# A Mamba-style block with a feed-forward on one core: when h, the second statistics, the ReLUs and y's transposes are issued

## The reference, cut to what matters

```python
x: (4, 4096, 512) float32;  D = 512, N = 16 states
mod = (silu(c) @ wmod).reshape(4, 6, 1, 512)      # sa, ca, ga, sb, cb, gb; ga, gb kept away from 0
h   = layernorm(x) * (1 + ca) + sa
x   = x + ga * attn(h)
h   = layernorm(x) * (1 + cb) + sb
x   = x + gb * ffn(h)

def attn(x):
    x_ssm, z = split(x @ w_in.T + b_in)
    z  = silu(z)
    dt = softplus(x_ssm @ w_dt.T + b_dt);  B = x_ssm @ w_B.T + b_B;  C = x_ssm @ w_C.T + b_C
    for every t:  s = exp(A * dt[t]) * s + dt[t] * B[t] * x_ssm[t];  y[t] = sum over N of s * C[t]
    y  = (y + D * x_ssm) * z
    return layernorm(y @ w_out.T + b_out + x) * gamma + beta

def ffn(x):
    s = x @ Win + bin                              # 64 columns
    g = sum over 16 inner units of relu(s * W1 + b1) * W2 + b2
    return g @ Wout + bout
```

## Time and profile before

| | us |
|---|---|
| median of three runs | 5229.29 |
| the profiled execution | 5223.79 |
| its span, first to last instruction | 5222.0 |
| PE busy, share of the span | 4803.0, 92% |
| ACT busy | 3842.9, 74% |
| DVE busy | 3730.8, 71% |
| POOL busy | 3372.6, 65% |
| mean granted TensorE clock | 0.968 |

### The profile page before, as it was taken

One profiled execution on the slowest core, in us unless ns is written; L12 is line 12 of the kernel. 1 busy time (PEld: TensorE's weight loads), 2 busy tenths in 40 slices (PEclk: granted clock), 3 DMA queues, 4 the chain that ended last, 5 costly groups with the idle time before them and its releaser, 6 DMA issues. The chain is left out here.

```text
span 5222.0 us, 76452 instructions
## 1 busy us (share of the span) xinstructions
PE 4803.0 (92%) x25664; PEld 3246.3 (62%) x25664; DVE 3730.8 (71%) x5163; ACT 3842.9 (74%) x6371; POOL 3372.6 (65%) x2699
## 2 busy tenths in 40 slices
PE   5889999999999999999999999999999999999997
PEld 3566666666666666666666666666666666666665
DVE  2577777777777777777777777777777777777775
ACT  0677877777877777877777777778777778777775
POOL 0566666666676666676666666666666666666674
PEclk8999999999999999999999999999999999999999
DMA  3111111111111111111111111111111111111111
GB/s 121 41 45 51 45 45 43 51 50 53 39 54 45 51 52 53 37 51 43 51 51 53 43 49 43 52 51 50 40 44 56 53 51 45 44 43 51 51 45 39
DMA packets 140649, 258.70 MB, mean 50 GB/s; under 512 B 18593, under 2 KB 18593, under 8 KB 140258
## 3 DMA queue, kind: packets, MB, share of 16 engines
q1 hardware_dynamic: 140258, 253.82, 15.4%
HBM read 216.01 MB, written 37.75 MB: 49 GB/s over the span
## 5 line engine op out<-in xcount | busy, mean ns | idle before, releaser
L336 POOL TENSOR_TENSOR work<-work,c_bc 128x512 f32<-128x512 f32 x2048 | 2592.8, 1277 | 1516.7 <-DVE work L1005 1147.5
L1005 DVE TENSOR_TENSOR_SCAN work<-work,state,b_ps 128x512 f32<-128x512 f32 x1792 | 2261.6, 1275 | 648.0 <-PE b_ps L404 605.2
L770 ACT ACTIVATE work<-u_td,b_td 128x512 f32<-128x512 f32 x2048 | 1453.7, 710 | 404.4 <-PE b_ps L404 401.1
L444 PEld LDWEIGHTS y_ps<-ident,work 128*128 128x128 f32 x8192 | 1019.7, 143 | 805.2 <-issue 719.0
L404 PE MATMUL b_ps<-ident,work 128*128 128x128 f32 x8192 | 1276.3, 280 | 250.3 <-DVE work L1005 133.4
L760 ACT ACTIVATE work<-dt_t,neg_a 128x512 f32<-128x512 f32 x2048 | 1451.0, 709 | 45.5 <-DVE work L1005 45.5
L444 PE MATMUL y_ps<-ident,work 128*128 128x128 f32 x8192 | 1234.4, 276 | 0.0
L404 PEld LDWEIGHTS b_ps<-ident,work 128*128 128x128 f32 x8192 | 980.5, 144 | 341.7 <-DVE work L1005 162.8
L596 PE MATMUL dense<-h_t,w_in_t 128*128 128x512 f32 x1024 | 534.3, 614 | 1.1 <-DVE u_td L1086 1.1
L508 PE MATMUL dense<-w_out_t,proj 128*128 128x512 f32 x1024 | 533.1, 614 | 0.0
L535 PE MATMUL dense<-h_t,w_in_t 128*128 128x512 f32 x1024 | 505.6, 597 | 6.6 <-ACT h_t L774 6.1
(11 more groups left out here) (92 smaller groups left out, 4665.6 us busy)
## 6 DMA issues: line engine op xcount, KB each, us to landing
c_bc<-c_d SPq DMA_DIRECT2D x512, 256.0 KB, 3.2
xn<-in_x SPq DMA_DIRECT2D x128, 256.0 KB, 5.0
x<-in_x SPq DMA_DIRECT2D x128, 256.0 KB, 3.7
out_dram<-x SPq DMA_DIRECT2D x128, 256.0 KB, 2.1
work<-in_wmod SPq DMA_DIRECT2D x6, 1024.0 KB, 7.5
par_d<-work SPq DMA_DIRECT2D x4, 768.0 KB, 3.3
w_in_t<-in_w_in_t SPq DMA_DIRECT2D x1, 2048.0 KB, 15.0
gain_shift<-par_d SPq DMA_DIRECT2D x4, 512.0 KB, 4.7
```

Of the source, the lines that this page charges most:

```text
L336: gp.tensor_tensor(pr[:, (s * U + i) % PR_RING, :], hs[:, (s * U + i) % HS_RING, :], c_bc[:, (s * N + n) % C_RING, :], ALU.mult).then_inc( ...
L444: last = mm(y_ps[:, tb, j * P:(j + 1) * P], pr[:, (s * U + i) % PR_RING, tb * P:(tb + 1) * P], ident[:, :], is_transpose=True, start=(i == ...
L770: A(v[:, n % V_RING, tb, :], u_td[:, s % 2, tb, :], ACT.Copy, scale=b_td[:, s % 2, tb, n:n + 1]).then_inc(S["v_done"], 1)
L1005: V.tensor_tensor_scan(hs[:, (s * U + i) % HS_RING, :], decay[:, (s * U + i) % DEC_RING, :], b_ps[:, i % 2, :], state[:, i:i + 1] if s % N ...
```

## The change

Four things move; no instruction that computes is added or removed.

- A semaphore `res_used` is counted up after each `add_residual`. `front`'s h waits for four of these instead of for `pre_ps`.
- `SECOND` becomes units 19, 22, 26, 28.
- `feed_forward` is split: the first two ReLUs of a chunk (`first_relus`) are issued at units 62 and 63 of the step before, the other six at units 0, 0, 1, 2, 2, 3. The last z block's sigmoid moves to units 3, 4, 5, and POOL's `last_gate` to unit 6.
- In `ORDER`, `yz.0` goes ahead of `g.6` and `yz.1` ahead of `g.7`; `dense` follows.

```diff
--- before.py
+++ after.py
@@ -26,7 +26,7 @@
 
 
 
-    ORDER = """g.0 g.1 g.2 g.3 g.4 g.5 g.6 yz.0 g.7 yz.1
+    ORDER = """g.0 g.1 g.2 g.3 g.4 g.5 yz.0 g.6 yz.1 g.7
         res.0 yz.2 pre.0.0 yz.3 pre.0.1 pre.0.2 out.0 pre.0.3
         res.1 pre.1.0 out.1 pre.1.1 pre.1.2 out.2 pre.1.3
         res.2 pre.2.0 out.3 pre.2.1 sk.0 pre.2.2 sk.1 pre.2.3
@@ -63,7 +63,7 @@
         return int(END[".".join(str(n) for n in part)] * U / TOTAL)
 
 
-    SECOND = [made("pre", tb, 3) + 5 for tb in range(TB)]
+    SECOND = [made("pre", tb, 3) + (5 if tb == TB - 1 else 9 - tb) for tb in range(TB)]
 
     ctx = ExitStack()
     with ctx:
@@ -159,7 +159,7 @@
         PER = {
             "SP": dict(stored_0=Q, stored_1=Q, stored_2=Q, stored_3=Q, c_stored=Q),
             "Pool": dict(prod_done=U, xsh_done=TB, x1_done=TB, dt_done=KD, u_done=KD, sz_done=KD),
-            "PE": dict(b_made=U, y_added=U, skip_added=KD, s_ps=1, g_used=J, yz_ps=KD, out_ps=TB, pre_ps=TB, xt_ps=KD, xs_ps=KD,
+            "PE": dict(b_made=U, y_added=U, skip_added=KD, s_ps=1, g_used=J, yz_ps=KD, out_ps=TB, res_used=TB, pre_ps=TB, xt_ps=KD, xs_ps=KD,
                        cb_ps=1, bt_ps=1, x2_ps=KD, dt_ps=KD, z_ps=KD, ut_ps=TB),
             "ACT": dict(dec_done=U, v_done=N * TB, rel_done=J, gm_done=1, lnp_done=TB, rstdp_done=TB,
                         lnx_done=1, rstdx_done=1, ln2_done=1, rstd2_done=1, t2_done=TB, xn_done=TB,
@@ -375,7 +375,7 @@
                     gate(s, m)
 
             def last_gate(b):
-                yield 3
+                yield 6
                 gate(b, KD - 1)
 
             def step(s, has_s, has_f, has_b, has_c):
@@ -499,8 +499,9 @@
                     mm(to[:, j * P:(j + 1) * P], b_out_t[:, j, :], ident[:, :], is_transpose=True,
                        start=(j == 0), stop=False)
                 for j in range(KD):
-                    mm(to[:, j * P:(j + 1) * P], h_t[:, b % 2, j, tb * P:(tb + 1) * P], ident[:, :],
-                       is_transpose=True, start=False, stop=False)
+                    last = mm(to[:, j * P:(j + 1) * P], h_t[:, b % 2, j, tb * P:(tb + 1) * P], ident[:, :],
+                              is_transpose=True, start=False, stop=False)
+                last.then_inc(S["res_used"], 1)
 
             def add_pre(s, b, tb, k):
                 if tb == 0:
@@ -624,15 +625,12 @@
             def dense(s, has_s, has_f, has_b, has_c):
                 f, b, c = s + 1, s - 1, s - 2
                 for k in range(J):
-                    if has_b and k == J - 1:
-                        yield slot("yz", 0)
-                        turn_y(s, b, c, 0)
+                    if has_b and k >= J - 2:
+                        yield slot("yz", k - J + 2)
+                        turn_y(s, b, c, k - J + 2)
                     if has_c:
                         yield slot("g", k)
                         add_g(s, c, k)
-                if has_b:
-                    yield slot("yz", 1)
-                    turn_y(s, b, c, 1)
                 for tb in range(TB):
                     if has_b:
                         yield slot("res", tb)
@@ -774,19 +772,27 @@
                 A(dst, psum, ACT.Identity, scale=mod[:, scale, g:g + 1], bias=mod[:, shift, g:g + 1]
                   ).then_inc(S[done], 1)
 
-            def feed_forward(s, b, c):
-                for j in range(J):
-                    yield (0, 0, 1, 1, 2, 3, 3, 4)[j]
-                    if j == 0:
-                        act.wait_ge(S["s_copied"], at("s_copied", c, 1))
-                        act.wait_ge(S["dt_done"], at("dt_done", s, 1))
-                    elif j < RELU_RING:
-                        act.wait_ge(S["sz_done"], at("sz_done", b, j + 1))
-                        act.wait_ge(S["x1_done"], at("x1_done", c, j + 1))
-                    else:
-                        act.wait_ge(S["g_used"], at("g_used", c, j + 1 - RELU_RING))
-                    A(tmp[:, j % RELU_RING, :], gm[:, :], ACT.Relu, scale=w1[:, j:j + 1], bias=b1[:, j:j + 1]
-                      ).then_inc(S["rel_done"], 1)
+            def relu(c, j):
+                if j == 0:
+                    act.wait_ge(S["s_copied"], at("s_copied", c, 1))
+                    act.wait_ge(S["dt_done"], at("dt_done", c + 2, 1))
+                elif j < RELU_RING:
+                    act.wait_ge(S["sz_done"], at("sz_done", c + 1, j + 1))
+                    act.wait_ge(S["x1_done"], at("x1_done", c, j + 1))
+                else:
+                    act.wait_ge(S["g_used"], at("g_used", c, j + 1 - RELU_RING))
+                A(tmp[:, j % RELU_RING, :], gm[:, :], ACT.Relu, scale=w1[:, j:j + 1], bias=b1[:, j:j + 1]
+                  ).then_inc(S["rel_done"], 1)
+
+            def first_relus(b):
+                for j in range(2):
+                    yield U - 2 + j
+                    relu(b, j)
+
+            def feed_forward(s, c):
+                for j in range(2, J):
+                    yield (0, 0, 1, 2, 2, 3)[j - 2]
+                    relu(c, j)
                 yield made("g", J - 1)
                 act.wait_ge(S["g_used"], at("g_used", c, J))
                 act.wait_ge(S["rel_done"], at("rel_done", c, J))
@@ -853,7 +859,7 @@
                 for j in range(KD):
                     yield made("xt", j)
                     act.wait_ge(S["xt_ps"], at("xt_ps", f, j + 1))
-                    act.wait_ge(S["pre_ps"], at("pre_ps", f - 2, TB))
+                    act.wait_ge(S["res_used"], at("res_used", f - 2, TB))
                     modulate(h_t[:, f % 2, j, :], inside(s, ("pre.3", "z.0", "z.0", "xs.0")[j])[:, :], f // NC, KD + j, j,
                              "h_done")
                 for m in range(KD):
@@ -906,9 +912,9 @@
                 if has_f:
                     chains.append(front(s, f))
                 if has_c:
-                    chains.append(feed_forward(s, b, c))
+                    chains.append(feed_forward(s, c))
                 if has_b:
-                    chains += [sigmoid(b, KD - 1, 0), second(s, b), attend(b), normalize_second(f, b)]
+                    chains += [sigmoid(b, KD - 1, 3), first_relus(b), second(s, b), attend(b), normalize_second(f, b)]
                 if has_f:
                     chains += [softplus(f), normalize(f)]
                 if has_s:
```

## The result

The changed kernel takes 4860.91 us (median of four runs, 4860.24 to 4861.48); before it was 5230.0 beside it. The ratio is 0.9295, with a 95% interval of 0.9279 to 0.9311. The forecast was 4896, the range 4855 to 4990. The profiled execution took 4860.24 us, its span is 4858.5.

A forecast was written before the change was run, and what follows sets the result against it. PE was taken as the bound; per steady step -3.33 - 3.66 - 3.2 - 1.2 + 0.4 = -11.0 us, times 29 is -319, with the other steps -334: 4890 us profiled, 4896 as median, range 4855 to 4990.

The forecast's parts named there:

- What bounds the kernel: Steady steps: PE is the bound, so its waits, 10.1 us of a 157.7 us step, lengthen the span.
- `h` waits for `res_used`: Unit 23, `front`'s first `h`: ACT then waits only for `xt.0`, saving 3.66 us a step.
- B: PE's stall at unit 23, behind ACT's `h` waiting for `pre_ps`: 3.66 us lost per steady step, all to go.
- Statistics of `x1`: Unit 17: statistics moved to units 19, 22, 26, 28 let scan 16 follow scan 15, saving 3.33 us a step.
- The clock: Behind the stalls at units 17 and 23: no stall, no fall to the lower clock, saving 3.2 us a step.
- A: PE's stall at unit 17, with DVE's statistics waiting for POOL's `x1`: 3.33 us lost per steady step, all to go.
- The start of the step: Up to residual 0: earlier ReLUs and `yz.0` save 1.35 us by count, 1.2 taken; new wait for `y` copies 1.4.
- What is late next: ACT's chain from `h`(1) to `h`(2): PE waits 0.55 us instead of 0.17, adding 0.4 us a step.
- Cooling by the new wait: Rival, step's start: the new 1.4 us wait lowers the clock, costing 1.7 to 3.4 us a step; 4945 to 4995; 14%.
- Waits coming back: Rival, DVE or ACT: thin margins at scan 27, `h`(2) or POOL's gate cost 1 to 3 us a step; 10%.
- A staying: Rival, units 18 to 22: PE meets POOL's product and two additions, 150 us come back, 5045 us; 3%.
- a late gate: Rival, step's start: the later sigmoid blocks POOL's gate of z.3, DVE waits at `yz.3`; slower, 5275 us; 3%.

The follow-up runs named there:

- old_relus: The changed kernel with ReLUs, last sigmoid and last gate back where they were before, the new order of `yz` and `g` kept: 4869.7 us.
- h_alone: The kernel before with only the wait of `h` changed from `pre_ps` to `res_used`: 5057.4 us, ratio 0.9674.
- stats_alone: The kernel before with only the statistics of `x1` moved to units 19, 22, 26, 28: 5070.0 us, ratio 0.9700.
- no_start: The changed kernel with the step's start as before (ReLUs, last sigmoid, last gate and order back): 4906.8 us.
- start_alone: The kernel before with only the step's start changed (ReLUs, last sigmoid, last gate, order of `yz` and `g`): 5195.8 us, ratio 0.9936.
- stats_16: The changed kernel with the first statistics of `x1` at unit 16 instead of 19: 4908.9 us.

## Why the prediction was right, and where it was off

*What bounds the kernel:* right. Where waits of PE went and no others came, the time fell by at least as much. The idle time is not the whole price, though: old_relus has even less of it in its steady steps than the change (4238.60 - 4155.23 = 83.4 us against 85.5) and is 9 us slower. Its ReLU waits come in 60 pieces where the wait for the copies came in 29.

*`h` waits for `res_used`:* right; B went whole, and h_alone shows it without the rest. ACT waits 0.36 us for the transposes ahead of `h`(0), where it had stood for 8.20.

*Statistics of `x1`:* right; stats_alone. The margin was real but thin: at unit 17 the same statistics cost 11 us, at unit 16 48.

*The clock:* right in kind and nearly in size. Alone, B's removal is worth 168.5 / 30 = 5.6 us a step and A's 155.9 / 31 = 5.0, of which 3.66 and 3.33 are lost in the stalls themselves; so 2.0 and 1.7 us are left for the clock, where the prediction had 3.2 for the two together. These 3.7 us also hold the small delays named below.

*The start of the step:* right, and counted to 0.1 us. The count gave 1.35, I took 1.2. Measured is 1.4: residual 0 starts 2201.10 - 2186.70 = 14.40 us into the step before, and 2201.17 - 2188.20 = 12.97 us into it after. Its chain is this:

```profile
...
2193.84 1.29 DVE L1043 COPY dt_t<-y_ps 128x512 f32<-128x512 f32 x2 [0.83 <-PE y_ps L444]
...
2196.23 1.26 DVE L1043 COPY dt_t<-y_ps 128x512 f32<-128x512 f32 x2
...
2197.55 0.66 PE L404 MATMUL dense<-ident,dt_t 128*128 128x128 f32 x4 [1.25 <-DVE dt_t L1043]
...
2198.64 0.68 DVE L1049 TENSOR_TENSOR proj<-sz_t,dense 128x512 f32<-128x512 f32 x1
...
2200.43 0.67 DVE L1049 TENSOR_TENSOR proj<-sz_t,dense 128x512 f32<-128x512 f32 x1
...
2201.17 0.64 PE L499 MATMUL dense<-ident,b_out_t 128*128 128x128 f32 x4
```

PE waits 1.25 us for the copies, forecast were some 1.4, and residual 0 starts 0.07 us behind the second product. What I had not seen is that ReLUs and order are two ways to the same gain.

*What is late next:* here the sum had its error. The chain is as described:

```profile
...
2246.43 0.78 ACT L772 ACTIVATE h_t<-dense,mod 128x512 f32<-128x512 f32 x1 [1.78 <-PE dense L404]
...
2248.82 0.60 PE L404 MATMUL dense<-ident,xn 128*128 128x128 f32 x4
...
2250.73 0.76 ACT L772 ACTIVATE h_t<-dense,mod 128x512 f32<-128x512 f32 x1
...
2251.55 1.12 PE L536 MATMUL dense<-h_t,w_in_t 128*128 128x512 f32 x2 [0.39 <-ACT h_t L772]
```

From the second `h` (2246.43) to `xs.0.0` ACT is the later one, and PE waits 0.39 us; 0.55 was forecast. But I added 0.4 us a step for it, against an average step of before whose clock loss I had taken from the step of 154.5 us. That step, at full clock, had this same wait already:

```profile
...
1945.86 1.13 PE L535 MATMUL dense<-h_t,w_in_t 128*128 128x512 f32 x2 [0.43 <-ACT h_t L774]
```

So 0.4 was counted twice. With it the account closes: 0.4 for `h`, 0.2 for the start taken under its count, and about 0.3 of small delays that vanished with A and B (laid beside a step of no_start, the step of 154.5 us loses 0.05 us at the restart behind each, and 0.2 ahead of unit 22's `turn_v`) make 0.9 of the 0.95 us between -11.0 and -11.95; times 29 that is 28 us. All that lies outside these 29 steps gave (5222.0 - 4858.5) - (4573.5 - 4226.7) = 16.7 us instead of 15. That makes 30 us, which is what lies between the profiled execution of the change, 4860.2, and the 4890 forecast for it. The other 5 of the 35 us lie between there and the median: I carried over the 5.5 us by which the median of before stands above its profiled execution, and after the change the two are 0.7 us apart.

*The rivals.* Cooling by the new wait did not come: 1.25 us in one piece left the clock at 1.00 in all 29 steps. In step 1, where PE waits 2.89 us for the copies in the changed kernel, until 305.81, the clock did fall, to the lower level:

```profile
...
306.50:309.50 3.00, 2.81 (x13) 2.12 (x11) 2.98 (x5) 2.41 (x5) 1.28 (x1) 0.50 0.27 87
```

Waits coming back, A staying, a late gate: none. The Trainium skill's rule that matmul busy time is no measure of nearness to the limit (Perfetto Trace Analysis, "Identifying the Most-Contended Engine") is no objection here: PE was the bound with its weight loads at 62% busy, and it works without a gap for 43 us with them at 28.81 of 43.00 us, 67%. This PE is full at that number. (The prediction speaks of transposes for 43 us on end; the stretch holds matmuls of 512 columns too.)

## What to carry to other kernels

Where one engine is full in the dense stretches, each of its waits is worth its length, and a long one more, for the clock behind it; find for each what ended it, and then what stood ahead of that in its own queue. A wait on a late event (all of `pre`, where the last reader was the residual) costs nothing on its engine and all on what is queued behind it. When a price is taken as the difference of two steps, look up which waits the cheaper step holds before adding another for the same wait.

## What the runs showed of the hardware

What the lower clock costs depends on more than the length of the stall. In the trace of before stalls of 3.15 and 3.50 us left one steady step of 29 at a clock of 1.00, and stalls of 3.05 to 3.19 and 3.50 us cost the average step 3.2 us. With A alone (h_alone) 9 of the 29 steps stayed at 1.00, with B alone (stats_alone) 5. Moving the start of the step by 1.4 us made start_alone lose some 20 us more in the span, with the same stalls. Waits of 1.25 us (the change) and 1.0 us (stats_16) never lowered it in a steady step. A shorter stall than A did so outside them: behind one of 2.57 us in before (PE restarts at 5106.46) the clock was 0.50 from 5107 to 5110 us. The Trainium skill (TensorE: Matmul & The Clock Gate, "The HAM clock gate") says that the instant at which the clock changes varies from run to run against the start of the kernel. This case agrees so far as steps of the same work took 154.5 and 157.2 us, and runs of start_alone 5185.1 to 5196.8.
